# ACT's copies behind the exponentials, POOL's second power behind the splits, and the router's bit split in three pieces

## The reference, cut to what matters

```python
def balanced_assignment(scores):            # 8192 tokens, 8 experts, C = 1024
    for e in range(E):
        s = jnp.where(taken, -jnp.inf, scores[:, e])
        _, idx = jax.lax.top_k(s, C)
        parts.append(idx); taken = taken.at[idx].set(True)
...
q = rms_norm(proj(Wq), qn_w); k = rms_norm(proj(Wk), kn_w); v = proj(Wv)
attn = softmax(einsum('bhnd,bhmd->bhnm', q, k) * scale)
out = einsum('bhnm,bhmd->bhnd', attn, v) ... @ Wo.T
...
x = x + attention(xn) + ffn(xn)             # xn = layernorm(x)
```

## Time and profile before

| | |
|---|---|
| median of 3 runs | 1125.38 us (1125.14 to 1126.7) |
| the profiled execution, its time | 1120.88 us |
| the profiled execution, its span | 1119.1 us |
| granted TensorE clock, mean | 0.982 |
| PE busy | 1049.3 us, 94% of the span |
| DVE, ACT, POOL busy | 834.2, 740.1, 734.6 us |
| chain that ended last | PE 69%, DVE 9%, issue 7%, POOL 7% |
| the longest wait by line | ACT L628 for PE's scores, 123.8 us in 172 waits |

### The profile page before, as it was taken

One profiled execution on the slowest core, in us unless ns is written; L12 is line 12 of the kernel. 1 busy time (PEld: TensorE's weight loads), 2 busy tenths in 40 slices (PEclk: granted clock), 3 DMA queues, 4 the chain that ended last, 5 costly groups with the idle time before them and its releaser, 6 DMA issues.

```text
span 1119.1 us, 20945 instructions
## 1 busy us (share of the span) xinstructions
PE 1049.3 (94%) x7222; PEld 680.7 (61%) x7222; DVE 834.2 (75%) x1847; ACT 740.1 (66%) x956; POOL 734.6 (66%) x768
## 2 busy tenths in 40 slices
PE   4599999989999999999999996899999999999997
PEld 3344554444444544544454442378999889998897
DVE  6799998567777778786877688588677687676861
ACT  1188887768888877888888884765455555554550
POOL 3678878657677776766766758655676656767334
PEclk9699999999999999999999997999999999999999
DMA  3579669555757667558676774414334343344313
GB/s 121 113 162 189 166 145 219 115 120 151 152 115 179 120 140 165 136 133 170 140 151 126 172 151 133 138 57 118 81 86 114 69 120 81 82 101 80 70 20 38
DMA packets 86345, 138.16 MB, mean 123 GB/s; under 512 B 12752, under 2 KB 38608, under 8 KB 86224
## 3 DMA queue, kind: packets, MB, share of 16 engines
q1 hardware_dynamic: 57936, 103.85, 41.1%
q0 software_dynamic: 12288, 16.79, 9.0%
q10 hardware_dynamic: 16000, 15.99, 5.5%
HBM read 86.25 MB, written 50.33 MB: 122 GB/s over the span
## 4 chain that ended last, share of the span: by engine, by line
PE 69%; DVE 9%; issue 7%; POOL 7%; DMA 3%; ACT 3%; SPq 1%; ACTq 0%; POOLq 0%; DVEq 0%
PE W L1365 16%; PE S L1351 16%; PE pv L461 13%; PE S L446 10%; PE W L407 7%; PE W L418 3%; DMA stq<-parts 2%; ACT prob L628 2%; PE W L432 2%; DVE xb L695 1%; SPq L305 1%; POOL hi L1105 1%; PE R L381 1%; DVE ssq L747 1%; DVE raw L740 1%
## 5 line engine op out<-in xcount | busy, mean ns | idle before, releaser
L628 ACT ACTIVATE prob<-S 128x1024 f32<-128x1024 f32 x512 | 498.0, 1022 | 124.9 <-PE S L446 123.8
L461 PE MATMUL pv<-prob,v 128*17 128x512 f32 x2048 | 249.3, 604 | 1.7 <-DVE oT L773 1.7
L446 PE MATMUL S<-stq,stk 64*128 64x512 f32 x1024 | 201.3, 459 | 19.4 <-ACT prob L628 14.9
L446 PEld LDWEIGHTS S<-stq,stk 64*128 64x128 f32 x1024 | 84.4, 186 | 142.7 <-ACT prob L628 111.9
L1627 POOL DMA_INDIRECT out<-prob,order_rows x64 | 106.1, 1657 | 48.0 <-DVE prob L1567 37.1
L1087 POOL TENSOR_TENSOR sq<-raw 128x512 f32<-128x512 f32 x64 | 66.5, 1040 | 93.1 <-DVE raw L740 61.5
L461 PEld LDWEIGHTS pv<-prob,v 128*17 128x17 f32 x2048 | 47.9, 97 | 123.6 <-issue 119.1
L1427 ACT ACTIVATE wq_act<-S,b 128x512 f32<-128x512 f32 x64 | 44.0, 687 | 93.9 <-PE S L1351 93.6
L1351 PE MATMUL S<-raw_nT,xT_w 128*128 128x512 f32 x384 | 91.1, 395 | 1.7 <-DVE raw_nT L1545 1.7
L1109 POOL TENSOR_TENSOR lo<-full,hi 128x512 fp32r<-128x512 f32 x64 | 82.6, 1290 | 5.1
L1351 PEld LDWEIGHTS S<-raw_nT,xT_w 128*128 128x128 f32 x384 | 71.7, 189 | 19.4 <-issue 3.5
(11 more groups left out here) (247 smaller groups left out, 2651.4 us busy)
## 6 DMA issues: line engine op xcount, KB each, us to landing
stk<-parts SPq DMA_DIRECT2D x192, 128.0 KB, 4.2
stq<-parts SPq DMA_DIRECT2D x192, 128.0 KB, 6.5
parts<-hi SPq DMA_DIRECT2D x64, 256.0 KB, 2.1
parts<-lo SPq DMA_DIRECT2D x64, 256.0 KB, 2.0
xT<-in_w SPq DMA_DIRECT2D x32, 512.0 KB, 5.0
out<-ao ACTq DMA_DIRECT2D x32, 256.0 KB, 4.8
xb<-in_x ACTq DMA_DIRECT2D x13, 512.0 KB, 4.9
xb<-in_x SPq DMA_DIRECT2D x3, 512.0 KB, 5.0
```

Of the source, the lines that this page charges most:

```text
L446: ins = e.matmul(S[n % 2][:, h, :], stack["k"][u][64 * h:64 * h + 64, p, c * P:(c + 1) * P], stack["q"][u][64 * h:64 * h + 64, p, :], star ...
L461: ins = e.matmul(pv[32 * j:32 * j + VW, :], v[b % 2][:, c, 8 * u + 4 * g + j, :], prob[(2 * t + j // 2) % RING][:, j % 2, :], start=(c == ...
L628: e.activation(prob[n % RING][:, :, :], S[n % 2][:, :, :], ACT.Exp).then_inc(s_exp, 1)
```

## The change

It moves instructions and cuts one step into three; it adds 12 short DVE instructions and no other.

```diff
@@ scalar_program, in each period
-                if scored(at - 2) is not None:
-                    evict_xT(e, scored(at - 2), 0)
+                softmax(e, 4 * at)
                 if scored(at - 3) is not None:
                     evict_xT(e, scored(at - 3), 1)
                     if scored(at - 3) + XB < B:
                         load_x(e, scored(at - 3) + XB)
                 if b and kk in (5, 6):
                     evict_o(e, b - 1, kk - 5)
-                softmax(e, 4 * at)
                 for u in range(2):
                     if nb < B and squares_at(nb, u) + 1 == at:
                         inverse_rms(e, nb, u)
                 softmax(e, 4 * at + 1)
+                if scored(at - 2) is not None:
+                    evict_xT(e, scored(at - 2), 0)
+                softmax(e, 4 * at + 2)
                 if b and kk in (5, 6):
                     put_out(e, b - 1, kk - 5)
-                softmax(e, 4 * at + 2)
                 softmax(e, 4 * at + 3)
@@ gpsimd_program, in each period
                 if scored(at) is not None:
                     first_power(e, scored(at))
-                if scored(at - 1) is not None:
-                    second_power(e, scored(at - 1))
...
                 if b + 2 < B and kk == 5:
                     split_x(e, b + 2)
+                if scored(at - 1) is not None:
+                    second_power(e, scored(at - 1))
...
@@ vector_program
                 if at == ROUTE:
-                    split_scores(e)
+                    split_scores(e, 0)
...
+                if at in (ROUTE + 1, ROUTE + 2):
+                    split_scores(e, at - ROUTE)
@@ split_scores(e, n): the same six operations, on a slice of the experts
+        at = slice(*((0, 1), (1, 4), (4, E))[n])
...
@@ ask, before the first question of an expert other than the first
                 e.wait_ge(r_sel, 2 * ex)
+                e.wait_ge(r_split, 18)
```

More of the change, by code:

```diff
@@ L269, in attention_and_routing @@
     hot_e = [xb[0][:, i, :].bitcast(BF16).rearrange("p (t q) -> p t q", t=COLS) for i in range(2)]
-    word = xb[0][:, 0:2, :].rearrange("p c d -> p (c d)").bitcast(I32)
-    part = xb[1][:, 0:2, :].rearrange("p c d -> p (c d)").bitcast(I32)
+    word = xb[0][:, 0:2, :].rearrange("p c d -> p (c d)").bitcast(I32).rearrange("p (e t) -> p e t", e=E)
+    part = xb[1][:, 0:2, :].rearrange("p c d -> p (c d)").bitcast(I32).rearrange("p (e t) -> p e t", e=E)
     low = xb[2][:, 0:2, :].rearrange("p c d -> p (c d)").rearrange("p (e t) -> p e t", e=E)
@@ L796, in shift_vector, with split_scores @@
         e.tensor_tensor(sh[1][:, :], shf[:, :], sh[0][:, :].bitcast(F32), ALU.subtract).then_inc(g_shl, 1)
-    def split_scores(e):
-        words = scores[:, :, :].rearrange("p e t -> p (e t)")
-        e.wait_ge(s_score, B)
-        e.tensor_scalar(word, words.bitcast(I32), 31, 1, ALU.arith_shift_right, ALU.logical_shift_right).then_inc(r_split, 1)
-        e.wait_ge(r_split, 1)
-        e.tensor_tensor(word, word, words.bitcast(I32), ALU.bitwise_xor).then_inc(r_split, 1)
-        e.wait_ge(r_split, 2)
-        e.tensor_scalar(part, word, LOW_BITS, None, ALU.arith_shift_right).then_inc(r_split, 1)
-        e.wait_ge(r_split, 3)
-        e.tensor_scalar(words, part, UNIT, None, ALU.mult).then_inc(r_split, 1)
-        e.tensor_scalar(word, word, 2 ** LOW_BITS - 1, None, ALU.bitwise_and).then_inc(r_split, 1)
-        e.wait_ge(r_split, 5)
-        e.tensor_copy(low[:, :, :].rearrange("p e t -> p (e t)"), word).then_inc(r_split, 1)
+    def split_scores(e, n):
+        at = slice(*((0, 1), (1, 4), (4, E))[n])
+        bits, words, parts, lows = (t[:, at, :] for t in (word, scores.bitcast(I32), part, low))
+        if n == 0:
+            e.wait_ge(s_score, B)
+        e.tensor_scalar(bits, words, 31, 1, ALU.arith_shift_right, ALU.logical_shift_right).then_inc(r_split, 1)
+        e.wait_ge(r_split, 6 * n + 1)
+        e.tensor_tensor(bits, bits, words, ALU.bitwise_xor).then_inc(r_split, 1)
+        e.wait_ge(r_split, 6 * n + 2)
+        e.tensor_scalar(parts, bits, LOW_BITS, None, ALU.arith_shift_right).then_inc(r_split, 1)
+        e.wait_ge(r_split, 6 * n + 3)
+        e.tensor_scalar(scores[:, at, :], parts, UNIT, None, ALU.mult).then_inc(r_split, 1)
+        e.tensor_scalar(bits, bits, 2 ** LOW_BITS - 1, None, ALU.bitwise_and).then_inc(r_split, 1)
+        e.wait_ge(r_split, 6 * n + 5)
+        e.tensor_copy(lows, bits).then_inc(r_split, 1)
     def ask(e, ex, i):
```

## The result

The changed kernel takes 1134.4 us against 1125.64 us before, both medians of the runs: a ratio of 1.0077 with a 95% interval of 1.0061 to 1.0092, so it is slower by 8.8 us. I had forecast 1128.2 us, slower by 2.8. The sign was right, the size was three times too small, and the time lies outside my range of 1122.5 to 1132.5. One of the four executions of the changed kernel took 3377.9 us and is left out of the ratio; the other three took 1134.16 to 1134.57.

The account below looks back on a forecast made before the run. PE was taken as the bound in most periods, so only its waits count. Terms -4.4 + 1.6 + 4.8 + 1.2 less 0.4 gave +2.8 us, on the median of 1125.38 a forecast of 1128.2 us, range 1122.5 to 1132.5.

Parts of the forecast that it names:

- (a): Period 30: exponentials ahead of the eviction remove PE's waits and the half clock behind them, -4.4 us.
- (b): Split of scores in three pieces, periods 32 to 36: waits removed against pieces locked out by POOL, +1.6 us.
- The halves: Period 32's removed waits (-2.3) with the first piece (+1.2); the third piece (+2.4) with late hi and oT (+0.3).
- The wait of 2.4 us: Period 35: PE waits for the count because POOL locks out the third piece's DVE operations; 2.4 us, ends 0 and 3.4.
- The first piece: Period 32: two POOL lo delay its six DVE operations, so PE waits 0.6 us for the count and 0.6 for oT.
- (c): evict_o behind the first exponential, batches behind the pass: second exponential late, PE waits in kk 5 and 6, +4.8 us.
- (d): The pass: moved evictions cost nothing, second power behind the splits delays L706 and PE's turn; +1.2 us, ends 0 and +6.
- the clock falls again: Rival: the wait in period 35 is followed by a stretch at 1.2 GHz, +1.7 us, 1129.9 us; chance 0.1.
- Pieces are not locked out: Rival: POOL does not hold off the split's pieces, so 1124.2 us, no difference; chance 0.2.
- faster: Rival: late stacks absorb ACT's lateness in kk 5 and 6, split unlocked; -4.6 us, 1120.8 us; chance 0.12.
- L708 loses too: Rival: in the pass L708 also waits for the next POOL instruction, +6 instead of +1.2, 1133 us; chance 0.13.

Follow-up runs that it names:

- bef_xT: The kernel before with only evict_xT's two halves moved behind the first and second exponential; ratio 0.9960 to the kernel before.
- ctl_before: The kernel before run once more with no edit, as a control; ratio 0.9992 to the kernel before.
- best1: The kernel before with evict_xT's halves behind exponentials and the split in pieces, the third at the end of period 41; ratio 0.9945 to the kernel before.
- aft_pow_back: The changed kernel with POOL's second power put back ahead of squares and splits; ratio 1.0033 to the kernel before.
- aft_pow_cast: The changed kernel with POOL's second power ahead of the cast and xl in kk 5 only; ratio 1.0031 to the kernel before.
- aft_split_whole: The changed kernel with the scores split in one piece at the head of period 32, as before; ratio 1.0055 to the kernel before.
- best4: best1 with ACT's inverse_rms of kk 2 (lg and rs) moved behind the second exponential; ratio 0.9939 to the kernel before.

## Why the prediction was right in sign and wrong in size

The difference without head, interval 0 and tail is 9.3 us in the two profiles, near the 8.8 of the medians. Against the terms:

- **(a), -4.4 forecast.** Right: 4.2 us in intervals 29 and 30 of the change. The wait for xl went, the clock was 1.00. Without evict_o's lateness (bef_xT) the same intervals gave 4.96 us, and the 0.8 us between the two is the 0.8 of the forecast. That the ratio of (a) alone again says 4.5 is luck. Not foreseen: kk 4 of the pass gained 0.4 to 0.5 us three times.
- **(b), +1.6 forecast, +2.3 measured** (-2.5 and +4.7; 2.5 to 2.9 by undoing it). The halves were forecast at -1.1 and +2.7, so that the sum is nearer than its parts. The first half gained more since PE came to period 32 late by the stack, and its size hangs on the execution: against ctl_before it would be -4.2. The six operations were locked out one by one as worked out: "4.9 to 5.9 us" forecast, 5.3 measured. The wait of 2.4 us measured 2.71, since the answer's own L848 lost a POOL instruction too. The first piece cost 0.26 + 0.47 us in best1, 1.2 forecast. What failed here, as the second and smaller step, is that I kept the half clock behind that wait out of the sum, as a rival of chance 0.1. It came in five of five profiles that have the third piece there (interval 36: 6.44 to 7.15 us), 1.6 us or more each.
- **(c), +4.8 forecast, 5.0 to 5.4 by undoing it.** Right, step by step: the second exponential at 2.48 us, kk 6 by 0.50 us (0.45 forecast), kk 5 by 0.28 (0.25), and kk 5 of periods 45, 69 and 93 absorbed. The stack and count waits absorbed 2.9 us and not 1.4, and small costs in batches 14 and 15 made up for part of it. The 5.0 to 5.4 also hold 1.8 us in intervals 29 to 31 that this term did not count, less the 1.4 in 35 and 36.
- **(d), +1.2 less 0.4 forecast, 5.0 to 5.4 by undoing it.** This is the step that failed, by some 4 us, of which 1.5 (interval 0) have no shown cause. The prediction wrote "the power is harmless, and what now stands in its place is not", and then priced what stands in its place only for L706 and PE's turn. It did not go on down DVE's queue: L729 and L732 had run under the harmless power, and now run into xl, 1.7 us more in each kk 5. Behind them stand the sum of squares, then lg and rs on ACT, and then the second exponential of kk 6. Since DVE is busy for 92% of the pass, the lateness reaches the next batch's kk 3. The new wait of 1.93 us for the stack of period 32 begins in the same way, five periods earlier. In period 27 of the change POOL is 1.5 us later than in aft_pow_back, so that L729 there meets onl:

```profile
212.96 0.77 DVE L729 TENSOR_TENSOR sm<-sT,rstd 128x32 f32<-128x32 f32 x1
...
212.40 1.28 POOL L1133 TENSOR_TENSOR onl<-onf,onh 128x512 fp32r<-128x512 f32 x1
```

In aft_pow_back and aft_pow_cast the same L729 takes 0.19 us. Behind it, in the change, full, hi and lo come 0.6 us later, the last DMA of the stack is issued 0.9 us later than in aft_pow_back and lands 1.7 us later, while (a) has made the stack due 4 us sooner. Interval 31 is 5.84 to 7.29 us in the five profiles with this L729, and 5.50 and 5.21 in those two. The DMAs themselves also took longer to land in some executions (9.5 us for the last one in the change, 8.7 and 7.6 in those two); why stays open. Interval 0 is taken up in the last section. The upper end of the term, +6, would have held it, but for another reason (L708 losing its race), which did not happen: L708 kept 0.17 us in every batch of the change.

Of the rivals, "the clock falls again" was right as an addition. "Pieces are not locked out" and "faster" fall. "L708 loses too" had the right time, 1133, by the wrong instruction. The lock itself, which the Trainium skill states (SBUF — State Buffer, "Who interferes with whom"), holds for the integer pieces: L812 took 1.33 us beside raw and 0.29 with POOL waiting. That the second power does not take part, as the row said against the same section, holds too: L729 took 0.19 us beside it and 0.92 beside xl.

## What to carry to other kernels

When a step is moved on one engine, list what the other engine runs at the place that is left and at the new place, for its whole queue and down to the next wait of the bounding engine, not for the first victim alone; a step that costs nothing may be the cover of what follows. A chain of small dependent DVE operations belongs where POOL waits: look for POOL's idle time in the timeline first, cut the chain second. And a wait of PE is to be priced with the half clock that may follow: here waits of 2.6 to 3.2 us at the count of period 35 had it behind them in five profiles of five, and waits of 1.2 to 1.8 us at that of period 32 in three of four.

## What the runs showed that I had not expected

- The wait of PE for the count in period 32 was followed by a stretch at half clock in three profiles (ctl_before, bef_xT and aft_split_whole, waits of 1.77, 1.78 and 1.17 us, interval 33 at 6.96, 6.61 and 6.95 us) and not in the first profile of the kernel before (1.79 and 5.30 us). So the length of the wait does not decide it. It makes 1.7 us between executions of one kernel.
- Interval 0 took 5.84 to 6.05 us in the five profiles of kernels that have the power behind xl, and 4.55 to 4.57 us in the other nine; in the five a stretch at half clock took 3.1 to 3.4 us of it, in the nine none. aft_pow_cast, whose POOL queue is the same as the change's up to period 5, is among the nine. So the order of work does not explain it, and whether it is chance stays open. It would be 1.5 us of the 8.8, and of what undoing (d) gave back.
- Small shifts change which DVE operation meets a POOL instruction. In period 44 of best1 L866 took 1.30 us where the kernel before had 0.74 for the same operation, and PE waited 1.25 us for the count instead of 0.31. Timelines of DVE and PE, best1:

```profile
292.68 1.30 DVE L866 SCALAR_TENSOR_TENSOR tie<-rank,need,eq 128x64 f32<-128x64 f32 x1
...
297.97 0.20 PE L485 MATMUL R<-sel,below 128*128 128x64 bf16 x1 [1.25 <-DVE part_cnt L841]
```

Period 44 is 6.3 us long in all four of best1 to best4, which gives back 0.9 us of what they gain. The same operation is behind the 0.5 us of period 68 and the 0.65 of period 92 in the profiles of the kernel before and in bef_xT: 1.24 to 1.38 us where the period is long, 0.74 to 0.76 where it is not.
